# A four-layer gated cross-attention model: norms in groups of four tiles, keys and query weights made a stage ahead, prologue and first attention merged, rms from the variance

## The reference

```python
def _layernorm(x, axis=-1, eps=1e-05):
    return (x - mean) / sqrt(var + eps)

x = x + tanh(g_xattn[l]) * xattn_l(_layernorm(x), ctx_1024, ...)
x = x + tanh(g_ffn[l])   * ffn_l(_layernorm(x), ...)

def xattn(xn, ctx, Wq, bq, Wk, bk, Wv, bv, Wo, bo):       # 16 heads of 16
    scores = (xn @ Wq + bq) @ (ctx @ Wk + bk).T / sqrt(16) # 64 keys; per head
    return softmax(scores) @ (ctx @ Wv + bv) @ Wo + bo
...
# layer 0: scores + fside, no biases bq to bo; then, with y = xn + o @ Wo.T:
h = gelu(layer_norm(y, g1, be1) @ W1.T + b1, approximate=False)   # 1024 wide
return layer_norm(y + h @ W2.T + b2, g2, be2)
# ffn 0: top 2 of 8 linear experts, softmax weights
# ffn 1: top 2 of 8 experts, silu(x @ g) * (x @ u) @ d, 512 wide
# ffn 2: gated unit of 704, activations and weights in blockwise fp4
# layer 3: scores masked with -1e18; ffn 3:
normed = xn * rsqrt(mean(square(xn)) + 1e-08) * norm_weight
shared = relu(normed @ sw1 + sb1) @ sw2 + sb2                      # 1024 wide
# ... plus top 2 of 8 relu experts, 1024 wide, on normed; sigmoid router
```

## Time and profile before

| | |
|---|---|
| median of three runs | 1903.96 us |
| the profiled execution: time, span | 1905.01 us, 1903.3 us |
| TensorE matmul, weight load | 1440.6 us (76%), 1327.3 us (70%) |
| VectorE | 1352.5 us (71%) |
| ScalarE | 773.8 us (41%) |
| GpSimd | 375.1 us (20%) |
| granted TensorE clock, mean of the span | 0.871 |
| moved by DMA | 147.74 MB |

### The profile page before, as it was taken

One profiled execution on the slowest core, in us unless ns is written; L12 is line 12 of the kernel. 1 busy time (PEld: TensorE's weight loads), 2 busy tenths in 40 slices (PEclk: granted clock), 3 DMA queues, 4 the chain that ended last, 5 costly groups with the idle time before them and its releaser, 6 DMA issues. The chain is left out here.

```text
span 1903.3 us, 28120 instructions
## 1 busy us (share of the span) xinstructions
PE 1440.6 (76%) x10178; PEld 1327.3 (70%) x10178; DVE 1352.5 (71%) x2556; ACT 773.8 (41%) x1289; POOL 375.1 (20%) x256
## 2 busy tenths in 40 slices
PE   3586694589597379999379216986792899999995
PEld 3575593478487379999269116975682788999995
DVE  4687757557778657877378885995777676888882
ACT  2553320200454237777345002324452323766662
POOL 1000100000000027775200000000001002566652
PEclk9798797689899569999689658997896899999998
DMA  3022001000001147786200100000000104777773
GB/s 141 25 98 64 23 1 50 1 0 0 14 1 45 67 149 224 232 236 142 70 1 1 46 0 1 1 1 14 1 1 26 66 1 165 240 218 222 217 219 80
DMA packets 44863, 147.74 MB, mean 78 GB/s; under 512 B 10915, under 2 KB 24006, under 8 KB 34502
## 3 DMA queue, kind: packets, MB, share of 16 engines
q1 hardware_dynamic: 27110, 122.41, 18.5%
q0 software_dynamic: 17664, 24.13, 7.2%
HBM read 126.07 MB, written 22.54 MB: 78 GB/s over the span
## 5 line engine op out<-in xcount | busy, mean ns | idle before, releaser
L271 PE MATMUL PS<-RA 128*128 128x256 f32 (+4 forms) x6456 | 954.8, 308 | 72.6 <-DVE RA L359 21.4
L271 PEld LDWEIGHTS PS<-RA 128*128 128x128 f32 x6456 | 879.7, 194 | 125.7 <-DVE RA L359 21.4
L249 PE MATMUL PS<-ident,FA 128*128 128x128 f32 x288 | 62.4, 406 | 217.4 <-DVE FA L203 108.2
L249 PEld LDWEIGHTS PS<-ident,FA 128*128 128x128 f32 x288 | 55.7, 216 | 223.4 <-DVE FA L203 110.8
L1236 POOL DMA_INDIRECT Y<-normed_rows,KT x92 | 154.0, 1674 | 239.4 <-DVE KT L1049 171.7
L1247 POOL DMA_INDIRECT sum_rows<-Y,KT x92 | 164.5, 1788 | 147.3 <-ACT Y L1284 127.4
L232 POOL TENSOR_TENSOR rstd<-vareps,neghalf 128x8 f32<-128x8 f32 x18 | 31.8, 1766 | 737.0 <-DVE vareps L192 580.8
L716 PE MATMUL PS<-VBF,FA 128*128 128x136 f32 x1024 | 138.1, 289 | 4.5 <-ACT FA L557 4.5
L716 PEld LDWEIGHTS PS<-VBF,FA 128*128 128x128 f32 x1024 | 126.6, 195 | 10.3 <-ACT FA L557 6.7
L1310 DVE TENSOR_TENSOR RA<-FA,RA 128x2048 fp32r<-128x2048 f32 x46 | 105.3, 2289 | 20.2 <-ACT RA L1276 19.1
L1263 ACT ACTIVATE FA<-PS,unit_bias 128x256 f32<-128x256 f32 x184 | 77.6, 477 | 91.5 <-PE PS L271 81.0
(11 more groups left out here) (232 smaller groups left out, 1987.3 us busy)
## 6 DMA issues: line engine op xcount, KB each, us to landing
FA<-in_eup SPq DMA_DIRECT2D x46, 1024.0 KB
FA<-in_edown SPq DMA_DIRECT2D x23, 1024.0 KB
FA<-in_edown SPq DMA_DIRECT2D x23, 512.0 KB
...
```

Of the source, the lines that this page charges most:

```text
L249: ins = pe.transpose(self.bank(q, k)[:, j * P:(j + 1) * P], self.xn[:, GT * q + j, k * P:(k + 1) * P], ident[:, :])
L271: ins = pe.matmul(dst, stat(a, k), mov(b, k), start=(first and n == 0), stop=(last and n == len(todo) - 1))
```

## The change

Nothing in what is computed changes but the rounding.

- `Norm` works by four groups of four tiles. Each group has its own moments, root and increments; normed tiles go alternately to two quarters of the buffer (or straight to Y, where Y was filled by a copy), banks alternate by `g % 2`. VectorE takes two groups' moments, then mixes the norm of one group, moments of a later one and the split of the one before.
- rms: the mean square of a normed tile is var / (var + eps), so that the root of (var + eps) * 1e-8 + var takes in both norms; norm_weight becomes a scale per partition in the hi copy and lo split, and in the experts' copies of gathered rows.
- `Ahead(l)`: Wq's split and the masked keys of layer l are made in the phase before: layer 1's in the linear experts, layer 2's in `route`, layer 3's in the four-bit stage. VectorE makes one subtraction of 128x256 on the unmasked keys; ScalarE masks hi and lo together, 16 instructions.
- The prologue's work is in attention 0: weights come as layer 0's and the other three's, X in four loads, and projections stand between norm groups. Y takes the normed tiles directly.
- In the tile loop TensorE reads the queries from the large array; the 64 copies (L566) go.
- In the gelu stage GpSimd's two additions wait for the normed tiles of all groups, and VectorE waits for them at its first addition to Y. In `close_block` moments and closing alternate by groups, and the wait for the two rows stands behind the first group's moments.
- Layer 2's X comes back in four loads.

```diff
+    def bank(self, g, k):
+        return PS[:, KC * (g % 2) + k, :]
+    def vector_stats(self, dve, steps, g):
...
+        steps(ins)
+        ins = dve.tensor_scalar(vareps[:, ts], meanvar[:, ts, 1], EPS, None, ALU.add)
+        if self.rms:
+            steps(ins)
+            ins = dve.scalar_tensor_tensor(vareps[:, ts], vareps[:, ts], 1e-8, meanvar[:, ts, 1], ALU.mult, ALU.add)
+        ins.then_inc(self.stats_ready, 1)
+    def vector_norm(self, dve, steps, g):
+        dve.wait_ge(self.rstd_ready, self.groups + g + 1)
+        if self.xn is not Y:
+            dve.wait_ge(self.tp_ready, 1 + KC * (self.groups + max(g - 1, 0)))
...
+    def tensor(self, pe, g):
+        pe.wait_ge(self.xt_ready, 1 + KC * (self.groups + max(g - 1, 0)))
+        pe.wait_ge(self.xn_ready, self.groups + g + 1)
+        for k in range(KC):
+            for j in range(GT):
+                ins = pe.transpose(self.bank(g, k)[:, j * P:(j + 1) * P], self.normed(g, j)[:, 0, k * P:(k + 1) * P], ident[:, :])
+            ins.then_inc(self.tp_ready, 1)
...
-            steps(ins)
-            self.moments(dve, steps, [self.xn[:, j, :] for j in range(HT)], slot)
-            steps(dve.tensor_tensor(rms[:, :], meanvar[:, slot, :, 0], meanvar[:, slot, :, 0], ALU.mult))
-            dve.scalar_tensor_tensor(vareps[:, slot, :], rms[:, :], 1e-8, meanvar[:, slot, :, 1], ALU.add, ALU.add
-                                     ).then_inc(self.sq_ready, 1)
...
+class Ahead:
...
+        self.raw = fview((7168, 6144, 2048, 8192)[l], KC, D)
+        self.kts = rview((10240, 24064, 24064, 24064)[l], 2, KC, P)
+        self.kb = rview(24576, NB, 2, KC, SC)
+        self.wq_in, self.wq_hi, self.wq_ready = (shared("ah_" + n) for n in ("wqin", "wqhi", "wq"))
...
+    def scalar_query_weights(self, act):
+        act.wait_ge(self.wq_in, 16 * (self.l + 1))
+        act.activation(self.wq[:, 0], self.raw, ACT.Copy, scale=SCALE).then_inc(self.wq_hi, 1)
+    def scalar_keys_hi(self, act):
+        act.wait_ge(kv.keys_done, self.l + 1)
+        act.activation(self.kts[:, 0], KT[:, self.l], ACT.Copy).then_inc(self.kt_hi, 1)
+    def vector_keys_lo(self, dve):
+        dve.wait_ge(self.kt_hi, self.l + 1)
+        dve.tensor_tensor(self.kts[:, 1], KT[:, self.l], self.kts[:, 0].bitcast(F32), ALU.subtract).then_inc(self.kt_ready, 1)
+    def scalar_keys(self, act):
...
+        for h in range(HC):
             for b in range(NB):
+                act.activation(self.kb[:, b, :, :, h * S2:(h + 1) * S2], self.kts[:, :, :, b * S2:(b + 1) * S2].bitcast(F32),
+                               ACT.Copy, scale=headmask[:, h:h + 1])
...
-        def keys_and_values():
-                for k in range(KC):
-                    for h in range(HC):
-                        act.activation(kb[:, b, 0, k, h * S2:(h + 1) * S2], KT[:, l, k, b * S2:(b + 1) * S2], ACT.Copy,
-                                       scale=headmask[:, h:h + 1])
...
-            if slot.has(3):
-                t, p = slot.tile(3)
-                if slot.has(1):
-                    slot.wait(act, s_ready, 3, -1)
-                    act.sem_inc(held, 1)
-                act.activation(qt[:, p], qs[:, :, :, bass.ds(t * P, P)], ACT.Copy).then_inc(qt_ready, 1)
...
+            dve.sem_inc(norm.xt_ready, 1)
+            kv.vector_context(dve)
+            kv.vector_weights(dve, 0)
+            ahead[0].vector_query_weights(dve)
+            moments(0)
+            kv.vector_weights(dve, 1)
+            moments(1)
+            kv.vector_values(dve, 0)
+            norm.vector_norm(dve, steps, 0)
+            ahead[0].vector_keys_lo(dve)
+            kv.vector_weights(dve, 2)
+            moments(2)
+            norm.vector_norm(dve, steps, 1)
+            norm.vector_lo(dve, 0)
+            kv.vector_values(dve, 1)
+            kv.vector_weights(dve, 3)
+            moments(3)
+            norm.vector_norm(dve, steps, 2)
+            norm.vector_lo(dve, 1)
+            kv.vector_values(dve, 2)
+            dve.wait_ge(bq_ready, l + 1)
+            queries_lo(0)
+            kv.vector_values(dve, 3)
+            dve.wait_ge(kv.values_done, LAYERS)
             dve.sem_inc(bias_free, 2)
...
-            for k in range(KC):
-                for h in range(HC):
-                    ins = dve.scalar_tensor_tensor(kb[:, b, 1, k, h * S2:(h + 1) * S2], KT[:, l, k, b * S2:(b + 1) * S2],
-                                                   headmask[:, h:h + 1], kb[:, b, 0, k, h * S2:(h + 1) * S2].bitcast(F32),
-                                                   ALU.mult, ALU.subtract)
+            norm.vector_norm(dve, steps, 3)
+            norm.vector_lo(dve, 2)
+            queries_lo(1)
+            norm.vector_lo(dve, 3)
+            output_weights_lo()
+            queries_lo(2)
+            queries_lo(3)
+        else:
...
+            norm.vector_lo(dve, 3)
+            output_weights_lo()
+            queries_lo(2)
+            queries_lo(3)
+            dve.wait_ge(bo_in, 16 * l)
...
+        def queries(g):
+            pe.wait_ge(norm.xt_ready, 1 + KC * (norm.groups + g + 1))
+            if g == 0:
+                pe.wait_ge(ahead[l].wq_ready, l + 1)
+            if g >= 2:
+                pe.wait_ge(q_split, Q + KC * (g - 1))
+            elif first:
+                kv.free(pe, LAYERS + g)
+            for oc in range(KC):
+                split_matmuls(pe, PS[:, 4 + KC * (g % 2) + oc, :], range(KC), lambda a, k: wq[:, a, k, oc * P:(oc + 1) * P],
+                              lambda m, k: xt[:, m, k, g % 2, :]).then_inc(q_ready, 1)
+        norm.tensor(pe, 0)
+        if first:
+            kv.project(pe, 2)
+        norm.tensor(pe, 1)
+        if first:
+            kv.project(pe, 3)
+        queries(0)
+        norm.tensor(pe, 2)
+        queries(1)
+        norm.tensor(pe, 3)
+        queries(2)
+        queries(3)
...
-                            ins = pe.matmul(PS[:, 2 * p + r, k * COLS:(k + 1) * COLS], qt[rows, p, a, k, :],
+                            ins = pe.matmul(PS[:, 2 * p + r, k * COLS:(k + 1) * COLS], qs[rows, a, k, t * P:(t + 1) * P],
...
-phases += [prologue(), attention(0)]
+phases += [attention(0)]
...
-    for h in range(NH):
-        norm.vector_stats(dve, steps, h, h)
+    norm.vector_stats(dve, steps, 0)
+    norm.vector_stats(dve, steps, 1)
         meanwhile()
-    for h in range(NH):
-        norm.vector_norm(dve, steps, h, h)
-        norm.vector_lo(dve, h)
+    norm.vector_norm(dve, steps, 0)
+    norm.vector_stats(dve, steps, 2)
+    norm.vector_norm(dve, steps, 1)
+    norm.vector_lo(dve, 0)
+    norm.vector_stats(dve, steps, 3)
+    norm.vector_norm(dve, steps, 2)
+    norm.vector_lo(dve, 1)
+    norm.vector_norm(dve, steps, 3)
+    norm.vector_lo(dve, 2)
+    norm.vector_lo(dve, 3)
...
-def copy_xn(act, norm, h):
...
+                if gated:
+                    ins = act.activation(xt[q][:, 0].rearrange("p k t -> p (k t)"), PS[:, 0, :], ACT.Copy)
+                else:
+                    for k in range(KC):
+                        ins = act.activation(xt[q][:, 0, k, :], PS[:, 0, k * BR:(k + 1) * BR], ACT.Copy, scale=norm_weight[:, k:k + 1])
+                ins.then_inc(xt_hi, 1)
...
         if kind == "gelu":
+            pool.wait_ge(norm.xn_ready, norm.groups + NG)
             for h in range(NH):
-                pool.wait_ge(norm.xn_ready, norm.groups + GH * (h + 1))
                 y = Y[:, HT * h:HT * (h + 1), :]
                 pool.tensor_tensor(y, y, row[:, 2].unsqueeze(1).to_broadcast([P, HT, D]), ALU.add).then_inc(y_bias, 1)
...
-        if kind == "gelu":
-            dve.wait_ge(y_bias, NH)
...
                 if kind == "gelu":
+                    if n == 0:
+                        dve.wait_ge(y_bias, NH)
...
+        def close(g):
...
+        moments(0)
         for load in row_in:
             dve.wait_ge(*load)
         steps(dve.tensor_scalar(row, row, gates[:, 0:1], None, ALU.mult))
-        for h in range(NH):
-            x = X[:, HT * h:HT * (h + 1), :]
...
+        for g in range(NG):
+            if g + 1 < NG:
+                moments(g + 1)
+            close(g)
...
+        def quantise_xn(g):
+            norm.vector_norm(dve, steps, g)
+            dve.wait_ge(norm.xn_ready, norm.groups + g + 1)
+            Quantiser(steps, xn[:, GT * (g % 2):GT * (g % 2 + 1), :].rearrange("p t d -> p (t d)")).all()
+        quantise_xn(0)
+        for g in range(1, NG):
+            quantise_xn(g)
+            norm.vector_lo(dve, g - 1)
+        norm.vector_lo(dve, NG - 1)
```

725 lines of the change are left out of this document (377 added, 348 removed).

## The result

| | before | after |
|---|---|---|
| median | 1903.40 us (4 runs, 1901.91 to 1904.92) | 1812.12 us (4 runs, 1811.86 to 1816.57) |
| ratio | | 0.9526, 95% interval 0.9509 to 0.9543 |
| profiled execution, span | 1905.01, 1903.3 us | 1816.57, 1814.8 us |
| mean granted clock | 0.871 | 0.876 |

The account below looks back on a forecast made before the run. TensorE bounds the long loops, hardly touched; VectorE is the longest queue in the preparation at stage heads. Stage terms sum to -84.8 us, from 1905.0 to 1820.2, with the median 1.05 lower: 1819 us, range 1803 to 1840.

Parts of the forecast that it names:

- Heads of layers 1 to 3: First moments to first transposed probabilities take 31.4, 31.4 and 32.6 us; attention gains 14.0, 17.4 and 19.5.
- VectorE's list by fours: Layer 1's head: VectorE, working in fours, is through the first split at 9.9 us; its whole list sums to 22.5.
- TensorE's chain of queries: Layer 1's head: query groups and last transposes in one chain from 10.4 us, plus 1.8 for low clock; scores at 26.0.
- the keys' 6.3 us: VectorE's 32 key instructions (6.34 us) in front of layer 1's first scores leave the head because they run earlier.
- Layer 0: Layer 0 and prologue: first transposed probabilities at 61.7 us instead of 84.67, gain 23.0.
- Gelu stage: GpSimd's two b2 additions, back to back, hold the weight splits; TensorE starts at 39.9 us against 32.8: +7.1.
- the rival of more gain: Earlier loads, weight splits slipped between additions (-4.5), key copies at lower bound, no cold starts: 1805 us, chance 0.2.
- Closing: Closing the block: VectorE stands from 307.7 to 311.7 for the second row; X done at 336.4, not 331.05: +5.35.
- Relu stage, route: Relu stage loses its second pass and copy to Y, -20.5; route's norm writes Y without ScalarE's copies, -3.4.
- Linear experts: Norm of linear experts and router by fours takes 19.4 us, before 20.0: -0.6.
- Four-bit stage: Ahead work of 1.1 us and 20 more quantiser instructions, less 3.3 for round trips: +1.2, bounds -2 and +2.
- the rival of the low clock: Smaller TensorE bursts start more often at 1.2 GHz, two in each of four heads, 18 us: 1837, chance 0.14.

Follow-up runs that it names:

- the extra transposes: Changed kernel plus 20 unused identity transposes on TensorE in the four-bit stage and at the heads of layers 1 to 3: 1812.73 us.
- layer 0's keys: Changed kernel with ScalarE's 16 masked key copies of layer 0 moved in front of the first queries, value copies where the keys stood: 1804.10 us, ratio 0.9485.

## Why the prediction was right

- **Heads of layers 1 to 3.** Forecast 31.4, 31.4 and 32.6 us, measured 29.5, 30.2 and 30.9. VectorE's list by fours was right to the step (first products at 10.2 for 10.4), and so was the view that TensorE's chain of queries ends last. In layer 1 it was 1.9 us too long: first scores 24.4 us behind the moments for 26.0, since the one group at the lower level (granted clock 0.69 over it, 1.00 over the rest of the chain) cost 1.3 us (4.26 against 2.99) for 1.8, and each of the two later groups of transposes held the chain 0.8 for 1.05; from scores to transposes 5.1 for 5.4.
- **Why the keys paid.** The working took the keys' 6.3 us from the head because they run earlier. The place gave at most 1.4 us a head; the form gave 8 to 13. So the term fitted by a reason that was half wrong, and it was undersized: beside VectorE's 6.3 us the old form costs ScalarE's 32 copies, which the prediction took off the head without a price and which in layer 1 held TensorE 2.4 us; the slower scores behind the hole are 0.3.
- **Layer 0.** 64.5 for 61.7: the keys in front of the last queries, seen in the working, took 7.9 us for 7.2, and began late. VectorE's last split in front of them ended at 49.0 for 46.3: the second weights were split at 18.6 for 16.5, and behind the third values VectorE stood 4.7 us for 2.3. The last low query ended at 59.6 for 56.8. The stage missed by 1.4 only, because the loop behind was 1.4 shorter than before, by no term of the sum: luck.
- **Gelu stage.** The two additions hold the weight splits, as forecast. They started 26.7 us behind the moments, not 28.4, and one split ran between the two; hence +5.1 for +7.1. The runs price the hold at 5.4 us. VectorE slipped one split between the additions, not both as the rival of more gain had it.
- **Closing.** +5.5 for +5.35, with the wait of 3.8 us for 4.0.
- **Relu stage, route.** The second pass and the copies to Y went for what their rows said: 20.9 at the router products for 20.5, 4.2 for 3.4. The route stage as a whole is 6.7 shorter in this profile; the 2.5 behind the products are not shown to be the change's, since executions of the same code took up to 309.2 us, 3.3 below before.
- **Linear experts.** Router products 19.0 us behind the moments for 19.4, and 1.0 more behind them that no term had.
- **Four-bit stage.** The step that missed: the head is 0.3 us longer (1.2 forecast), but the loop lost 4.5 us, 3.8 of them in its first 35 us, where the granted clock was 0.78 and not 0.90 (in the first 12 us 0.64 and not 1.00) and the first two sets of 24 products took 6.51 and 5.69 us for 4.10 each. That is the rival of the low clock, in a loop instead of at a head. The other kernels' executions gave 242.7 to 247.0 us for the stage, all above the 240.7 of before, of which there is one profile. What lowers the clock there stays open: the extra transposes did not settle it.
- **The sum.** The gain was 3.7 us larger than forecast in the profile and 7 in the median. The misses partly cancel: layers 1 and 2, route, gelu and the linear experts came 9.7 us below their terms, four-bit and layer 0 5.0 above. No run parts the merged prologue (21.6 us in its stage) or the relu stage's second pass (19.9) from the rest of the change: for these two the cause rests on the rows and the order of the code.
- **Slower, grouping gains little.** No tile loop moved by more than 1.6 us: from first to last transposes 73.4 and 73.3 in layer 1, 74.4 and 73.4 in layer 2, so queries read in place cost nothing. Layer 3's is 1.5 longer in this profile, and as long as before (83.2) in that of layer 0's keys.
